# A one-core graph kernel: one source one-hot in four is made by GpSimd in the counting loop by eight

## What is computed

```python
msg = h_src[src]
agg = jax.ops.segment_sum(msg, dst, num_segments=n)
...
x = _layernorm(x + _L0_gnn_ref(x, ...), axis=-1)   # then L1, L2, L3 in the same way
```

## Time and profile before

| what | value |
|---|---|
| median of 3 runs | 1914.79 us (1913.35 to 1915.44) |
| the profiled execution | 1920.13 us, its span 1918.4 us |
| mean granted TensorE clock of the profiled execution | 0.964 |
| PE, PEld busy | 1755.1 us (91%), 1414.5 us (74%) |
| DVE, POOL, ACT busy | 957.2 us (50%), 494.4 us (26%), 482.1 us (25%) |
| L1555, source one-hots on DVE | 464, 162.6 us busy, mean 377 ns |
| L1560, target one-hots on DVE | 232, 68.5 us busy, mean 295 ns |
| L1015, PE products of one-hots | 464, 148.4 us busy, mean 320 ns |
| L1018, PE products of zeros | 431 recorded, 163.3 us busy, mean 387 ns |

### The profile page before, as it was taken

One profiled execution on the slowest core, in us unless ns is written; L12 is line 12 of the kernel. 1 busy time (PEld: TensorE's weight loads), 2 busy tenths in 40 slices (PEclk: granted clock), 3 DMA queues, 4 the chain that ended last, 5 costly groups with the idle time before them and its releaser, 6 DMA issues.

```text
span 1918.4 us, 35049 instructions
## 1 busy us (share of the span) xinstructions
PE 1755.1 (91%) x9445; PEld 1414.5 (74%) x9479; DVE 957.2 (50%) x2851; ACT 482.1 (25%) x1262; POOL 494.4 (26%) x899
## 2 busy tenths in 40 slices
PE   3999996999988999999999999999999699999971
PEld 2456665788878888788878877877777489899851
DVE  7877774444455411122211127767777544444466
ACT  0044554322223211122221111112212123222323
POOL 1022223211123200000000002217888843223214
PEclk7999997999999999999999999999999799999986
DMA  5068889999779888877768889997777499999981
GB/s 136 35 282 336 360 362 377 327 323 324 271 274 361 322 291 290 255 215 215 210 199 302 287 258 291 290 276 247 259 262 242 131 328 371 371 371 372 373 303 67
DMA packets 339452, 535.59 MB, mean 279 GB/s; under 512 B 17871, under 2 KB 275322, under 8 KB 332442
## 3 DMA queue, kind: packets, MB, share of 16 engines
q1 hardware_dynamic: 329514, 516.24, 80.2%
q0 software_dynamic: 7888, 17.23, 2.4%
q10 hardware_dynamic: 1952, 0.95, 0.3%
HBM read 405.95 MB, written 128.41 MB: 279 GB/s over the span
## 4 chain that ended last, share of the span: by engine, by line
PE 60%; SPq 11%; DMA 8%; issue 7%; POOL 6%; DVE 5%; DVEq 2%; ACT 1%; ACTq 0%; POOLq 0%
PE psum L1128 41%; PE psum L1225 4%; DMA blk<-counts_src_on_rows 4%; PE psum L1018 4%; PE psum L1015 3%; SPq L494 3%; SPq L508 2%; PE psum L600 2%; POOL expert_rows_in L1998 2%; POOL pick_and_gate_of_row L2015 2%; PE psum L1037 2%; SPq L500 2%; PE psum L612 1%; SPq L497 1%; SPq L504 1%
## 5 line engine op out<-in xcount | busy, mean ns | idle before, releaser
L1128 PE MATMUL psum<-xsa,blk 128*128 128x512 f32 x2500 | 640.0, 403 | 5.5 <-DVE xsa L1694 2.8
L1128 PEld LDWEIGHTS psum<-xsa,blk 128*128 128x128 f32 x2500 | 455.8, 189 | 95.7 <-issue 6.1
L1128 PE MATMUL psum<-xsb,blk 128*128 128x512 f32 (+1 forms) x1875 | 406.9, 366 | 14.4 <-DMA blk<-counts_src_on_rows 10.2
L1128 PEld LDWEIGHTS psum<-xsb,blk 128*128 128x128 f32 x1875 | 314.8, 189 | 68.9 <-issue 14.1
L1976 POOL TENSOR_SCALAR ve<-mv 128x1 f32<-128x1 f32 x75 | 16.8, 223 | 760.7 <-DVE mv L1670 760.7
L1555 DVE TENSOR_SCALAR onehots<-counts_scratch 128x348 bf16<-128x348 f16 x464 | 162.6, 377 | 64.1 <-issue 40.1
L600 PE MATMUL psum<-route,expert_weights 128*128 128x128 f32 x1296 | 166.1, 282 | 2.4 <-DVE route L712 2.0
L1015 PE MATMUL psum<-onehots 128*128 128x349 bf16 x464 | 148.4, 320 | 19.1 <-DVE onehots L1560 17.1
L1018 PE MATMUL psum<-zrow 128*128 128x512 bf16 x431 | 163.3, 387 | 0.0
L600 PEld LDWEIGHTS psum<-route,expert_weights 128*128 128x128 f32 x1296 | 154.3, 195 | 11.5 <-DVE route L712 2.7
L612 PE MATMUL psum<-expert_weights,route 128*128 128x256 f32 x648 | 153.4, 380 | 0.2 <-ACT route L666 0.2
(11 more groups left out here) (317 smaller groups left out, 2114.6 us busy)
## 6 DMA issues: line engine op xcount, KB each, us to landing
blk<-counts_src_on_rows SPq DMA_DIRECT2D x125, 832.0 KB, 6.0
blk<-counts_src_on_rows SPq DMA_DIRECT2D x125, 768.0 KB
expert_weights<-in_L_gnn_w SPq DMA_DIRECT2D x162, 512.0 KB
blk<-counts_dst_on_rows SPq DMA_DIRECT2D x50, 832.0 KB, 5.5
counts_dst_on_rows<-band_rows SPq DMA_DIRECT2D x25, 1600.0 KB, 5.6
blk<-counts_dst_on_rows SPq DMA_DIRECT2D x50, 768.0 KB
counts_src_on_rows<-blk SPq DMA_DIRECT2D x13, 1600.0 KB, 8.9
counts_src_on_rows<-rblk SPq DMA_DIRECT2D x12, 1600.0 KB, 9.5
```

Of the source, the lines that this page charges most:

```text
L1128: mm = e.matmul(o, blk[n][:, k * P:(k + 1) * P], XS[:, k, :, 0:Fw], start=(k == 0), stop=(k == T - 1 and not own), skip_group_check=True)
```

## The change

- In the loop by eight, DVE leaves out the source one-hots of the chunks 3 and 7. POOL makes them, in two buffers of their own (`one_s` has six buffers now). A function `lent_slot` says which chunk is lent.
- For each lent chunk POOL copies the chunk's column and weight into a small fixed buffer (`lent_keys`), waits for its own copy (`keys_taken`), waits until the buffer's last use is over (`onehots_used` at least k + n - 2), makes the one-hot, and adds 4 to `lent_ready`. PE waits for `lent_ready` at these chunks in place of `sources_ready`.
- So that one copy takes both keys, `scol` and `wcol` no longer are two arrays but the even and the odd elements of one, `source_keys`. DVE reads them so too, in both loops.
- In the loop by eight PE's product of zeros has 384 columns; in the loop by four it keeps 512.
- POOL's pipeline is written out for each band (`unrolled=True`): the lent one-hots of band b, the casts of band b-1, then a loop that raises the two counters over the second half (`none_lent`), and the read of the next band's table entry.

```diff
-        xsa = rg("onehots", [P, UNROLL * (FW + 2 + P)], BF16)
+        xsa = rg("onehots", [P, (UNROLL + 2) * (FW + 2) + UNROLL * P], BF16)
...
-        scol, at = view(xsb, at, EG * P, F32)
+        v, at = view(xsb, at, 2 * EG * P, F32)
+        source_keys = v.rearrange("p (c two) -> p c two", two=2)
+        scol, wcol = [source_keys[:, :, k] for k in range(2)]
+        v, at = view(xsb, at, 2 * 2, F32)
+        lent_keys = v.rearrange("p (n two) -> p n two", two=2)
...
-        wcol = src_rows
...
+        def lent_slot(n, by):
+
+            return UNROLL + n // UNROLL if by > UNROLL and n % UNROLL == UNROLL - 1 else None
...
-                            e.wait_ge(S("sources_ready"), k + n + 1)
-                            e.matmul(o, one_d[:, u, :], one_s[:, u, 0:FW + 1], start=False, stop=True,
+                            lent = lent_slot(n, by)
+                            e.wait_ge(S("sources_ready" if lent is None else "lent_ready"), k + n + 1)
+                            e.matmul(o, one_d[:, u, :], one_s[:, u if lent is None else lent, 0:FW + 1], start=False, stop=True,
                                      skip_group_check=True).then_inc(S("onehots_used"), 1)
 
-                            e.matmul(psum[:, par, 0:BANK], zrow[:, 0:P], zrow[:, 0:BANK], start=False, stop=True,
+                            fill = BANK if lent_slot(UNROLL - 1, by) is None else 3 * P
+                            e.matmul(psum[:, par, 0:fill], zrow[:, 0:P], zrow[:, 0:fill], start=False, stop=True,
                                      skip_group_check=True)
...
                 for n in range(by):
-                    c, u = chunk(n), n % UNROLL
+                    u = n % UNROLL
+                    if lent_slot(n, by) is not None:
+                        continue
+                    c = chunk(n)
...
-                                    ALU.is_equal, ALU.mult).then_inc(S("sources_ready"), 1)
+                                    ALU.is_equal, ALU.mult).then_inc(S("sources_ready"), 1 if lent_slot(n + 1, by) is None else 2)
...
-            pipeline(e, [(1, cast), (3, nothing)])
+            ends_of = [groups_of(e, 0), None]
+
+            def lent_sources(b, par):
+                own, before, middle, _ = ends_of[par]
+                with e.Fori(before, middle, 2 * UNROLL) as k:
+                    for n in range(UNROLL - 1, 2 * UNROLL, UNROLL):
+                        c, turn = chunk_index(k, own, n), n // UNROLL
+                        keys = lent_keys[:, turn, :]
+                        e.tensor_copy(keys, source_keys[:, bass.ds(c, 1), :].rearrange("p c two -> p (c two)"))\
+                            .then_inc(S("keys_taken"), UNROLL)
+
+                        e.wait_ge(S("keys_taken"), k + n + 1)
+                        carry_wait(e)
+                        e.wait_ge(S("onehots_used"), k + n - 2)
+                        carry_wait(e)
+                        e.tensor_scalar(one_s[:, lent_slot(n, 2 * UNROLL), 0:FW], iota_f, keys[:, 0:1], keys[:, 1:2],
+                                        ALU.is_equal, ALU.mult).then_inc(S("lent_ready"), UNROLL)
+
+            def none_lent(b, par):
+                _, _, middle, upto = ends_of[par]
+                e.wait_ge(S("lent_ready"), middle)
+                carry_wait(e)
+                with e.Fori(middle, upto, UNROLL) as k:
+                    e.sem_inc(S("keys_taken"), UNROLL)
+                    e.sem_inc(S("lent_ready"), UNROLL)
+                if b + 1 < T:
+                    ends_of[1 - par] = next_groups(e, b + 1, upto)
+            pipeline(e, [(0, lent_sources), (1, cast), (0, none_lent), (3, nothing)], unrolled=True)
```

More of the change, by code:

```diff
@@ L238, in gnn_program @@
         assert at <= 20480
-        wcol = src_rows
         one_w = FW + 2
-        one_s, at = view(xsa, 0, UNROLL * one_w, BF16)
-        one_s = one_s.rearrange("p (b s) -> p b s", b=UNROLL)
+        one_s, at = view(xsa, 0, (UNROLL + 2) * one_w, BF16)
+        one_s = one_s.rearrange("p (b s) -> p b s", b=UNROLL + 2)
         one_d, at = view(xsa, at, UNROLL * P, BF16)
         one_d = one_d.rearrange("p (b s) -> p b s", b=UNROLL)
-        assert at <= UNROLL * (FW + 2 + P)
+        assert at <= (UNROLL + 2) * (FW + 2) + UNROLL * P
         region.close()
@@ L383, in groups_of, with chunk_index @@
             return e.snap(e.to_reg((v & 511) - start), min_val=-(1 << 15), max_val=511), start, middle, upto
+        def lent_slot(n, by):
+            return UNROLL + n // UNROLL if by > UNROLL and n % UNROLL == UNROLL - 1 else None
+        def chunk_index(k, own, n):
+            return nc.s_assert_within(k + own + n, 0, EC + 3 * UNROLL,
+                                      skip_runtime_bounds_check_because="k runs from the band's start to its end")
         def next_groups(e, b, start):
@@ L1542, in chunk_loop @@
                 with e.Fori(ends[lo], ends[hi], by) as k:
[L1543 to L1546, removed]
+                    many(b, k, lambda n: chunk_index(k, own, n), by)
             lanes = [P, PAIR, P // 2, 2]
```

## The result

Four runs of the changed kernel took 1933.18 us in the median (1932.1 to 1934.91), beside 1914.07 (1912.66 to 1915.44) before: **19 us slower**, ratio 1.0096 with a 95% interval of 1.0083 to 1.0108. Forecast were 1919.0 and a range up to 1930, so the time lies above the range. The profiled execution has a span of 1930.0 us.

What follows compares the result with a forecast made beforehand. DVE's sequencer was taken to bound the long loop by eight, while short bands take turns. Terms 2.0 + 1.35 + 1.25 + 0.75 - 0.85 - 0.3 gave +4.2 us on 1914.8, thus 1919.0; range 1909 to 1930.

Steps and rivals of the forecast that it cites:

- The price of POOL's one-hot: Lent one-hot on POOL: 0.5 us taken from its copies' pace, 0.79 to 0.95 by its slow two-input operation.
- The term of +2.0 for the long turns: 18 long turns by eight, each 3.24 us and 0.11 more than before: +2.0 us (-1.3 to +4.1).
- PE waits for lent one-hots instead of DVE's: Rival: POOL needs over 3.2 us a turn by eight; at 3.5 us a turn 1929 us in all; chance 0.03.
- The rival in which they are free: Second register instructions queue while DVE's engine works, which sets the pace: turn by eight 2.98 us, 1909 in all; chance 0.16.
- The second register instruction: Each source one-hot with interleaved keys needs one more on DVE's sequencer: 0.09 us, bounds 0.06 and 0.11.
- The first turns by four: 25 turns behind digits and next to the casts, mostly waiting for PE: 0.03 us each, +0.75 (0 to +2).
- The further turns by four: 5 turns, no one-hot lost, four register instructions gained, 0.27 us each: +1.35 us (+0.9 to +2.2).
- The first turns by eight: 25 turns, one per band, a chain from PE's chunk 0 to the digits: +0.05 each, +1.25 us (-7 to +6).
- The zeros: Fewer zero columns for PE: nothing in long turns, -0.85 us where PE bounds at half clock, 35 to 41 us.
- POOL's hold on DVE: Time c each lent one-hot holds up DVE's engine: 0.2 us (0 to 0.7), hidden under the sequencer up to 0.38.
- The lock over a whole instruction: Rival: POOL shuts DVE out for its whole instruction, +11.7 us, 1927; 1943 at the two-input pace; chance 0.24.
- The clock: Forecast unchanged; rival: fewer zero columns make it fall to half in the long loop, about 1936 us; chance 0.04.

Runs made afterwards that it cites:

- e5_one_op: The changed kernel with POOL's one-hot made of the comparison alone, without the product with the weight: 1922.44 us against 1914.67, ratio 1.0037.
- e4_planes: The changed kernel with columns and weights as two planes of one array in place of interleaved: 1932.2 us against 1915.65, ratio 1.0091.
- e7_zeros_back: The changed kernel with 512 zero columns in both loops: 1931.99 us against 1914.67, ratio 1.0101.
- e1_keys: The kernel before with column and weight interleaved, nothing lent, 512 zero columns: 1931.0 us against 1915.65, ratio 1.0075.
- e11_spare: The kernel with one lent one-hot in eight, but DVE makes all eight and POOL's goes unread: 1917.28 us against 1914.68, ratio 1.0014.
- e12_one_128: The changed kernel with one lent one-hot in eight, keys in planes, 128 zero columns in both loops: 1907.38 us against 1915.79, ratio 0.9955.

## Why the prediction was wrong

**The price of POOL's one-hot: wrong, and the step that failed.** "I take 0.5, as it has one tensor input like the copy", with 0.95 as the end. It measured 1.63. Both rows behind the bounds were of other operations: a copy, and an operation of two tensors. Neither had two arithmetic steps with an operand from each partition, or 16-bit types, so the upper of them was no bound. The second step is worth 0.42 us (e5_one_op); why the comparison alone takes 1.21, no run shows. From it came "POOL needs 2.0 us a turn, hidden under 3.24": measured 4.28 and the bound. The term of +2.0 for the long turns measured +12.2; the run with 32 columns shows that it was this price alone. In the whole counting this price is some 20 us against that run, while undoing the interleaved keys (e4_planes) gave back 1 us by the medians.

**"PE waits for lent one-hots instead of DVE's"**, the rival at 0.03, is what happened, with its deciding point (over 3.2 us a turn) passed by far. It was priced at 3.5 us a turn from nothing. The number 4.28 also stood in the text, for a lock and a two-input pace; that it agrees is chance, since it was made of other parts.

**The count of turns** (43 and 30, 86 lent): right, 73 steps and 86 one-hots of POOL in the trace.

**DVE's sequencer as the bound of the long turn**: right. Its sum gave 3.09 with the measured price where 3.12 was measured, and eight second register instructions lengthened a turn by 0.53. The rival in which they are free fell.

**The second register instruction**: 0.09 forecast, 0.065 measured, in its bounds.

**The first turns by four**: wrong. "Mostly waiting for PE" gave +0.75; they measured +7.0, and +1.6 once the keys lay in planes. Four second register instructions at 0.065 are 0.26, and 0.28 is what each turn lost: all of it stood on the path of that turn. A part came back in the next turn: with the keys alone, the first turns by eight outside the one at half clock took 1.2 us less. The chain of waits of the changed kernel shows such a place, behind the digits and the reading of the table:

```profile
200.88 0.75 DVE digits L1602 x3
...
202.59 0.10 DVEq L1568
...
203.03 0.09 issue
203.12 0.10 DVEq L1568
...
203.47 0.09 DVEq L1568
203.57 0.29 DVE onehots L1573
203.86 0.12 issue
203.99 0.32 PE psum L1027
```

**The further turns by four**: +1.35 forecast, +1.8 measured.

**The first turns by eight**: +1.25 forecast, -3.6 measured, and in part luck of the clock: -3.2 is the one turn in which the kernel before ran at half clock, +1.8 the one in which the changed kernel did, and the other 23 took 2.3 less in all. In these the missing one-hots take more away (-10.7 in all with POOL's short one), and the late chunk 7 gives 7.1 back. The zeros have hardly a part in it: with 512 of them (e7_zeros_back) it is -2.7, and the difference lies in turns at half clock.

**The zeros**: "worth nothing" in long turns, right (3.13 to 3.11); -0.85 in all, too small when alone (3.2 us by the medians), and nothing that can be measured in the changed kernel.

**POOL's hold on DVE**: c = 0.2 taken, between 0.23 and 0.3 measured, under the 0.38 from which it decides. The lock over a whole instruction was the rival at 0.24. The Trainium skill (SBUF — State Buffer, section Who interferes with whom) has the other engine blocked fully for the whole instruction; the 0.37 us one-hot that DVE made at 46.02, inside POOL's 1.66 us from 45.41, does not fit that. Nor does it help to say that this form of instruction doesn't use the shared pair, as the same form was held at 46.52. The measurement decides.

**The clock**: unchanged in the long loop (1.00 from 41 to 69 us in both), as forecast, but not behind it. Before, then changed:

```profile
69.00:85.40 16.40, 12.75 (x55) 6.45 (x55) 11.02 (x39) 4.48 (x6) 2.66 (x4) 0.79 0.25 101
```

```profile
69.00:85.40 16.40, 10.80 (x59) 4.59 (x58) 12.12 (x37) 2.82 (x3) 12.32 (x14) 1.00 0.00 1
```

The difference helped the changed kernel by some 3 us in its trace, and its own stretch at 173 us cost it 1.8.

**The median and the counting**: the counting of one profiled execution gives +17.4 and the medians +19.1. For the keys alone it is +11.5 and +15.3, for the spare one-hot -1.5 and +2.6. The profiled execution of before was itself 5.3 us over its median, and part of that is its two turns at half clock. Another part lies behind the counting: the two profiled spans differ by 11.6 us only (1930.0 and 1918.4), so what comes after the counting took 5.8 us longer before. Without them, and without its own turn at half clock, the changed kernel's counting is 17.4 + 3.6 - 1.8 = 19.2 longer, e1_keys's 14.8 and e11_spare's 2.6, close to the medians. That fits, but with one trace of each kernel it is not shown.

## What to carry to other kernels

- Before work is lent to GpSimd, measure the very instruction there, with its number of steps and its operands: a copy's pace says nothing of it (0.19 + 0.84 ns an element against 1.63 us for 348). Then lend only as much as GpSimd does within the turn: with the keys in planes, two in eight lost 16.5 us, and one in eight gained 3.6, of which 3.2 are what fewer zeros gave alone. With 384 zeros in both loops the lending of one gained 5.0.
- Where the sequencer is the bound, an array's layout has a price: from two arrays or two planes of one, the two operands took one register instruction, interleaved they took two, and that alone was 15 us in a kernel of 1915. Why the interleaved ones take two is not shown.
- Two slow-downs of the same loop don't add; undoing either may show nothing until the other is gone. Make the cut in both directions.

## What was not expected of the hardware

- GpSimd's compare-and-multiply over 348 columns, 16-bit in and out, took 1.63 us; the compare alone 1.21; over 32 columns 0.53 (all medians).
- While it ran, most of VectorE's instructions kept their length; one or two of them were held by 0.15 to 0.3 us in all.
- A second address computation on VectorE's sequencer costs 0.065 us where the sequencer is the bound, less than its own neighbour of 93 ns.
- The granted clock fell to half for 3.4 to 10 us at different times between 75 and 292 us (not at all in e1_keys, from 228 us in e12_one_128), and those that can be priced cost 1.8 to 3 us. One trace of a kernel can carry several us of this.
